# Attention in pairs of steps instead of single steps, in a fused attention and feed-forward block

## The reference, cut to what matters

```python
q = (layernorm(x) @ Wq + bq).reshape(8, 512, 16, 16)      # B, S, H, DK
k = (ctx @ Wk + bk).reshape(8, 512, 16, 16)
v = (ctx @ Wv + bv).reshape(8, 512, 16, 16)
scores = einsum('bqhd,bkhd->hbqk', q, k) / sqrt(16)
attn = softmax(scores.reshape(16 * 8, 512, 512), axis=0)  # over head and batch together
out = einsum('hbqk,bkhd->bqhd', attn.reshape(16, 8, 512, 512), v)
x = x + tanh(g_xattn) * (out @ Wo + bo)
x = x + tanh(g_ffn) * ffn(layernorm(x))                   # quantised, 704 wide
```

## Time and profile before

| | us |
|---|---|
| median of 3 runs | 893.19 (891.55 to 894.06) |
| the profiled execution | 890.11 |
| its span, first to last instruction | 888.3 |
| attention stage, first scores (312.9) to last value products (742) | 429 |
| mean granted TensorE clock | 0.973 of full speed |

### The profile page before, as it was taken

How to read it: one execution, slowest core, us unless ns; L and a number is a source line. 1 busy time by engine, 2 the same in 40 slices (tenths; PEclk the granted TensorE clock), 3 DMA queues, 4 the chain that set the end, 5 groups by cost and what they waited for, 6 DMA issues and landing times. The chain is left out here.

```text
span 888.3 us, 20668 instructions
## 1 busy us (share of the span) xinstructions
PE 770.7 (87%) x8127; PEld 438.8 (49%) x8149; DVE 781.0 (88%) x1001; ACT 706.7 (80%) x1095; POOL 494.9 (56%) x353
## 2 busy tenths in 40 slices
PE   8897887877777688999889999999999989948977
PEld 6563361112212155666556666666666657714434
DVE  4799539999999979999799999999999995767968
ACT  3454449999999878899788999999999952768973
POOL 1333463000000017999898999999999996514500
PEclk9999999999999989999999999999999989969999
DMA  9796786565555567778776786768857566200014
GB/s 299 262 315 203 245 240 130 138 167 140 140 139 130 202 183 228 239 225 265 231 227 211 234 265 191 212 174 259 259 164 211 168 225 192 91 1 1 0 43 148
DMA packets 98094, 164.34 MB, mean 185 GB/s; under 512 B 9616, under 2 KB 37008, under 8 KB 97680
## 3 DMA queue, kind: packets, MB, share of 16 engines
q1 hardware_dynamic: 98000, 163.03, 61.5%
HBM read 133.63 MB, written 41.94 MB: 198 GB/s over the span
## 5 line engine op out<-in xcount | busy, mean ns | idle before, releaser
L978 POOL TENSOR_TENSOR e<-e,recip 128x768 f32<-128x768 f32 (+3 forms) x256 | 387.4, 1558 | 34.6 <-DVE recip L1020 34.6
L928 ACT ACTIVATE e<-ps_att 128x512 f32<-128x512 f32 x512 | 302.0, 648 | 36.6 <-PE ps_att L869 35.6
L1009 DVE TENSOR_REDUCE pair_sums<-e 128x128 f32<-128x2048 f32 x128 | 291.6, 2281 | 20.0 <-ACT e L928 19.6
L869 PE MATMUL ps_att<-arena 128*128 128x128 bf16 x2048 | 192.7, 220 | 0.3 <-issue 0.2
L884 PE MATMUL acc<-e,arena 128*32 128x128 f32 x4096 | 179.5, 294 | 11.7 <-DVE e L990 4.2
L869 PEld LDWEIGHTS ps_att<-arena 128*128 128x128 bf16 x2048 | 151.0, 98 | 58.8 <-issue 3.6
L694 ACT ACTIVATE copies<-ps_max 128x1024 bf16<-128x1024 f32 x189 | 175.6, 1087 | 0.0
L865 PE MATMUL ps_att<-shift,minus 128*128 128x512 bf16 x394 | 154.2, 391 | 14.9 <-DMA arena<-k_stack 9.2
L884 PEld LDWEIGHTS acc<-e,arena 128*32 128x32 f32 x4096 | 106.6, 111 | 40.7 <-POOL e L978 10.9
L709 DVE TENSOR_TENSOR high<-copies,high 128x3072 bf16<-128x3072 bf16 x63 | 110.0, 1745 | 0.4 <-ACT copies L694 0.4
L961 POOL CAST bo_parts<-arena 96x256 bf16<-96x256 f32 x1 | 0.4, 394 | 175.5 <-DMA arena<-in_L_xattn_bo_dram 175.5
(11 more groups left out here) (162 smaller groups left out, 879.0 us busy)
## 6 DMA issues: line engine op xcount, KB each, us to landing
arena<-k_stack SPq DMA_DIRECT2D x256, 256.0 KB, 3.3
arena<-q_stack SPq DMA_DIRECT2D x64, 256.0 KB, 4.2
k_stack<-parts SPq DMA_DIRECT2D x40, 256.0 KB, 3.5
q_stack<-parts SPq DMA_DIRECT2D x40, 256.0 KB, 3.6
k_stack<-k_stack SPq DMA_DIRECT2D x12, 512.0 KB, 10.9
arena<-in_x_dram SPq DMA_DIRECT2D x5, 1024.0 KB, 8.7
arena<-in_ctx_dram SPq DMA_DIRECT2D x4, 1024.0 KB, 6.5
arena<-q_stack SPq DMA_DIRECT2D x8, 512.0 KB, 8.0
```

The costliest lines, as they stand in the source:

```text
L869: last = nc.tensor.matmul(bank[:, j * P:(j + 1) * P], ks[:, i % KRING, b * P:(b + 1) * P], qs[:, h, b * P:(b + 1) * P], start=False, stop= ...
L928: nc.scalar.activation(e_at(qc * STEPS + i, half * HB, (half + 1) * HB).rearrange("p q b i -> p b q i"), ps[(qc * (2 * STEPS) + 2 * i + ha ...
L978: nc.gpsimd.tensor_tensor(part, part, by_pairs(recip[:, kc % 2, :], share), ALU.mult).then_inc(pool_scaled, 1)
L1009: nc.vector.tensor_reduce(pair_sums[:, :, h // 2, :], e[:, g % RING // 2].rearrange("p q s b i -> p q i (s b)"), AX.X, ALU.add).then_inc(s ...
```

## The change

- The unit of PE's order, of the ring, of the scaling and of the semaphores becomes the pair. PE does the four halves of two steps' scores, then the products of a whole pair (16 f32 matmuls, 32 records), 10 pairs behind. `e` is a ring of 11 pairs: the same memory and the same addresses within it.
- DVE and POOL scale a pair with one instruction each: POOL 8 blocks of 16 in the first pair of a region, 12 in the seventh, else 13; in the last region 6.
- DVE sums two pairs in one instruction, three times a region, and one pair twice, where a group of two would run over the ring's end one by one; the last sum has 5 or 6 parts instead of 8. DVE scales ahead of each sum, 8 pairs after the pair's exponentials.
- ACT's copies of `acc` stand behind pairs 4, 6, 8 and 10 of a chunk instead of steps 10, 14, 18 and 22.
- The shift of every fourth half is written by ACT as before, from the same half on.

```diff
-    LAG = 20
-    SLAG = 17
-    RING = 22
+    CHUNK = NC * PAIRS
+    ALL_PAIRS = NC * CHUNK
+    LAG = 10
+    RING = 11
+    BLOCKS = 2 * B
...
-    GATHER_AT = [LAG - H + BANK_HEADS * (j + 1) + 2 for j in range(BANKS)]
+    BANK_PAIRS = BANK_HEADS // 2
+    GATHER_AT = [LAG - PAIRS + BANK_PAIRS * (j + 1) for j in range(BANKS)]
...
-        return 7 if i % 4 == 1 else 6
+    POOL_BLOCKS = (8, 13, 13, 13, 13, 13, 12, 13)
+    END_BLOCKS = 6
+    GROUPS = ((0, 1), (2, 3), (4, 5), (6,), (7,))
+    def pool_share(p):
+        return END_BLOCKS if p >= ALL_PAIRS - PAIRS else POOL_BLOCKS[p % PAIRS]
...
-    FIRST_PRESET = 2 * LAG + 3
+    FIRST_PRESET = 4 * LAG + 3
...
-        e = sb("e", [P, RING // 2, QP, 2, B, 2])
-        pair_sums = sb("pair_sums", [P, QP, PAIRS, 2])
+        e = sb("e", [P, RING, QP, BLOCKS, 2])
+        partial = sb("partial", [P, QP, len(GROUPS) + 1, 2])
...
-                    for i in range(STEPS):
-                        for half in range(2):
-                            scores(qc, i, half)
-                        if LAG <= i < LAG + H and (i - LAG) % BANK_HEADS == 0:
-                            j = (i - LAG) // BANK_HEADS
+                    for j in range(CHUNK):
+                        for half in range(4):
+                            scores(qc, 2 * j + half // 2, half % 2)
+                        if LAG <= j < LAG + PAIRS and (j - LAG) % BANK_PAIRS == 0:
+                            bank = (j - LAG) // BANK_PAIRS
                             if not first:
-                                pe.wait_ge(gathered, BANKS * (qc - 1) + j + 1)
-                            clear(j)
-                        if i >= LAG or not first:
-                            for half in range(2):
-                                times_v(qc * STEPS + i - LAG, half)
+                                pe.wait_ge(gathered, BANKS * (qc - 1) + bank + 1)
+                            clear(bank)
+                        if j >= LAG or not first:
+                            times_v(qc * CHUNK + j - LAG)
...
+                        if p >= RING:
+                            act.wait_ge(multiplied, p - RING + 1)
+                        for half in range(4):
+                            n = 4 * p + half
+                            act.wait_ge(scored, n + 1)
                             nc.scalar.activation(
-                                e_at(qc * STEPS + i, half * HB, (half + 1) * HB).rearrange("p q b i -> p b q i"),
+                                e_at(p, half * HB, (half + 1) * HB).rearrange("p q z i -> p z q i"),
...
                             if preset(n + SCORES):
                                 act.wait_ge(exped, n + 1)
...
+                def add_up(p, n, k):
+                    dve.wait_ge(exped, 4 * (p + n))
+                    t = p % RING
+                    nc.vector.tensor_reduce(partial[:, :, k, :], e[:, t:t + n].rearrange("p t q z i -> p q i t z"),
+                                            AX.XY, ALU.add).then_inc(sum_done, 1)
...
+                for r in range(NC * NC):
+                    for k, (p, n) in enumerate(groups(r)):
...
+                            if p % PAIRS < PAIRS - 1:
+                                for i in range(n):
+                                    scale(p + i - PAIRS)
+                                if p % PAIRS + n == PAIRS - 1:
+                                    scale(p + n - PAIRS)
+                        add_up(p, n, k)
+                    invert(r, len(list(groups(r))))
```

More of the change, by code:

```diff
@@ L872, in scores, with times_v @@
                     last.then_inc(scored, 1)
[L874 to L888, removed]
+                def times_v(p):
+                    pe.wait_ge(pool_scaled, p + 1)
+                    pe.wait_ge(dve_scaled, p + 1)
+                    kc, pair = p % CHUNK // PAIRS, p % PAIRS
+                    for odd in range(2):
+                        for b in range(B):
+                            col = (pair * 2 + b // HB) * P
+                            grp = 32 * (b % HB)
+                            v_col = pair * 3 * DK + DK * odd
+                            z = odd * B + b
+                            last = nc.tensor.matmul(acc[grp:grp + 32, col:col + P], vpad[:, kc, b, v_col:v_col + 32],
+                                                    e_at(p, z, z + 1), start=False, stop=False,
+                                                    skip_group_check=True)
+                    last.then_inc(multiplied, 1)
                 def clear(j):
@@ L909, in _ @@
                     chunk(qc, False)
-                for g in range(ALL - LAG, ALL):
-                    for half in range(2):
-                        times_v(g, half)
+                for p in range(ALL_PAIRS - LAG, ALL_PAIRS):
+                    times_v(p)
             @block.scalar
@@ L921, in chunk @@
                 def chunk(qc, first):
[L922 to L927, removed]
-                            nc.scalar.activation(
-                                e_at(qc * STEPS + i, half * HB, (half + 1) * HB).rearrange("p q b i -> p b q i"),
[L930 to L933, removed]
+                    for j in range(CHUNK):
+                        p = qc * CHUNK + j
+                        if p >= RING:
[3 more added lines that the diff above has]
+                            act.wait_ge(scored, n + 1)
+                            nc.scalar.activation(
+                                e_at(p, half * HB, (half + 1) * HB).rearrange("p q z i -> p z q i"),
+                                ps[n % SCORES][:].rearrange("p (z q i) -> p z q i", z=HB, i=2),
+                                ACT.Exp, scale=DK ** -0.5).then_inc(exped, 1)
                             if preset(n + SCORES):
@@ L1024, in _, with scale @@
[L1024 to L1029, removed]
+                def scale(p):
+                    r = p // PAIRS
+                    if p % PAIRS == 0:
+                        dve.wait_ge(recip_copied, r + 1)
+                    share = pool_share(p)
+                    part = e_at(p, share, BLOCKS)
+                    nc.vector.tensor_tensor(part, part, by_pairs(recip_v[:, (r % 2) * P:(r % 2 + 1) * P], BLOCKS - share),
+                                            ALU.mult).then_inc(dve_scaled, 1)
@@ L1032, in ffn @@
+                for p in range(ALL_PAIRS - PAIRS, ALL_PAIRS):
+                    scale(p)
 def ffn(nc, sem, x, out_parts, out, keep):
```

100 lines of the change are left out of this document (41 added, 59 removed).

## The result

The changed kernel takes 933.62 us (930.14 to 934.12) against 892.54 for the kernel before in the same measurements: a ratio of 1.045, 95% interval 1.042 to 1.047. That is 41.1 us slower. The forecast was 945, 52.5 more than before, with a range from 929 to 958. The profiled execution of the changed kernel took 934.12, that of before 890.11.

What follows compares the result with a forecast made beforehand. Bound: a loop over PE and ACT, 3.12 us a pair; the moved half adds 0.50, so 3.62 x 117 = 423.5, with disturbances 435.8 against 383.35; with drain +52.7 on 890.1 to 893.19, forecast 945, range 929 to 958.

Steps and rivals of the forecast that it cites:

- The bound: Attention stage: a loop over PE and ACT through ACT's shift copy sets the pair, 3.10 us, 3.12 measured.
- The moved half of the products: First-step products, 16 records, move behind the last quarter of scores onto the loop: 0.50 us a pair, 0.41 to 0.77.
- s0: First of the four quarters of a pair's scores on PE; starts the loop, 0.71 us before E0.
- The pair: Attention stage, loop period of one pair (two steps): 3.12 + 0.50 = 3.62 us, times 117 = 423.5.
- E0: ACT's exponential of s0; the shift copy stands right behind it, counted 0.70 us later in the loop.
- Disturbances: Window beyond the loop: clears 3.3, filling 2.0, late K tiles 6, others 1 us; 18.3 before the change.
- Turns: PE's switches between scores and products: one each way a pair goes, where PE waits anyway; priced at 0.
- region starts: Starts of 8-pair regions, where products wait for scaled numbers: those stalls go, 2.5 us on DVE alone before.
- rival C: DVE's two-pair sums run at half the rate: 4.9 us a pair, near 1090 us; chance 0.03.
- rival A: Work of the engines is the pace, POOL fullest at 2.94 us a pair: faster, 865 us; chance 0.05.
- Rival B: PE's clock falls as PE idles about 0.7 us in each pair: about 1020 us; chance 0.05.
- Drain: End of the attention stage, POOL's last scalings and the last products: nothing moves much, +0.2 us.

Runs made afterwards that it cites:

- e2: Kernel before with only PE's order changed: four quarters of scores, then the products of two steps; 930.36 us, ratio 1.043.
- e4: Changed kernel with ACT's shift copy moved behind the pair's second exponential, for the next pair's first quarter; 877.94 us, ratio 0.985.
- e6: Changed kernel with the products of each pair's first step computed a second time, between second and third quarter of scores; 941.69 us, ratio 1.057.
- e9: Kernel before with ACT's shift copy moved behind the second exponential, for the next pair's first quarter; 882.12 us, ratio 0.987.
- e3: Changed kernel without ACT's copy of the shift, PE writing every shift; 886.18 us, ratio 0.992.
- e8: Kernel before without ACT's copy of the shift, PE writing every shift; 899.62 us, ratio 1.008.
- e1: Changed kernel with PE's old order, first-step products back between second and third quarter of scores; scaling, sums and ring by pairs; 897.59 us, ratio 1.008.
- e7: Like e6, but the second computation reads a fixed tile, 128 numbers in a row, instead of the ring; 931.96 us, ratio 1.045.
- e10: Like e7, but the fixed tile is read in the ring's own steps, 64 pieces 128 bytes apart; 932.76 us, ratio 1.046.

## Why the prediction was right, and where it was off

- **The bound.** Right: a loop over PE and ACT through the copy of the shift. e2 shows it with PE's order alone, e4 by moving the copy alone, and e6 by giving PE 23% more work for 8 us. In the kernel before the loop bound by little: with the copy moved there, most pairs took 3.00 to 3.03 (e9) instead of 3.12.
- **The moved half of the products.** Forecast 0.50, measured 0.49 (1.12 instead of 0.63 from products to s0). The nearest row, products behind products in the drain, was the right price. The stated high end, 0.77, did not go into the range, which took 0.55 without a reason; with 0.77 its upper end would have been some 26 us higher.
- **The pair.** Forecast 3.62, measured 3.56: the term that was mis-sized. The step "0.71 + 0.70 + 0.60 + 0.15 + 0.31 + 0.63" was carried over with its 0.70 from E0 to S. That number contained a slowdown of E0 by the very products that the change takes away from beside it; it became 0.65. 0.06 x 117 = 7 us of the 11 too many. What E0 gained there the last exponential lost: E3, now beside the products, has a median of 0.68 instead of 0.63 over pairs 11 to 126, but it is not on the loop. ACT's waits for scores, forecast near 76, came to 85.2.
- **Disturbances.** Forecast 12.3 in the window, measured 425.15 - 117 x 3.56 = 8.6. Waits for late K tiles are down from 9.7 to 3.8 (the earlier trace rows counts weight loads, and so does this row of the changed kernel; I had kept 6):

```profile
PEld ps_att L882 <- DMA arena<-k_stack: 3.8, 3, 1.6
```

  Filling: pair 10 lasted 6.20 (forecast 5.6). A clear costs 0.22 (pairs of 3.78 instead of 3.56), as priced.
- **Turns, DVE, POOL, ring, region starts.** All priced at nothing under the longer loop: right, no engine is over 85% busy in the window, and from 342 on the products never wait for DVE. A two-pair sum takes 4.42, less than two of 2.28; rival C did not come true. The rule of the Trainium skill (VectorE: DVE Perf Modes, section on the TRN2 errata), that larger tiles save their fixed part, agrees with 2 x 2.28 - 4.42 = 0.14 a merged sum; it decided nothing while the loop was the bound, as rival A would have needed.
- **Rival B, the clock.** The granted clock was 1.00 in mid-stage with PE idle 0.62 in each pair. Within the window it fell only in pairs 10 and 11, to 0.83 and 0.84: PE sat idle 1.62 before the products of pair 10 (the view names DVE, but the scaling that ended last, at 341.16, was POOL's), and the shift after them took 0.61 instead of 0.39. The oscillation that the Trainium skill describes for banks used in turn (TensorE: Matmul & The Clock Gate, section on psum-queue depth-cycling) does not show at these gaps in mid-stage.

```profile
341.22 1.93 PE L902 MATMUL acc<-e,arena 128*32 128x128 f32 x32 [1.62 <-DVE e L1002]
343.09 0.61 PE L882 MATMUL ps_att<-shift,minus 128*128 128x512 bf16 x1
```

- **Drain.** Forecast +0.2, measured -0.2.
- **The base.** I had added nearly all of the 3.1 us by which the profiled execution of before lay under its median. That of the changed kernel lies at its median's upper side (934.12 against 933.62), so the profiled executions differ by 44.0, the medians by 41.1. Of the 44.0, the window has 41.8; 2.3 lie behind the attention stage, where 148.25 us passed instead of 145.94 although the change touches nothing there. That the window alone comes so near to the 41.1 of the medians is in part chance.

## What to carry to other kernels

When all engines look 90% full, follow one period of the timeline from an instruction back to itself: each step from one release to the next is a term, and as long as that loop sets the pace only work on it has a price. Merging steps to save turns or fixed costs can move work from beside a wait to behind it. So look first for the wait that the merged work would land behind, here that for a 0.6 us copy by another engine. Moving that copy to where its result is needed one period later made the kernel before 0.9 to 1.3% faster and the changed kernel about 6%. The change by pairs itself cost 4.5% with the copy where it was, gained 1.5% without any copy (e3 against e8), and could not be told from nothing with the copy moved.

## What the runs showed of the hardware

The first exponential of a pair (128x512 f32, from PSUM into the ring in SBUF) had a median of 0.69 to 0.71 us over pairs 11 to 126 where it ran beside products that read the ring (before, e1, e6), and of 0.62 to 0.63 beside products that read another tile (e7, e10) or beside none (the changed kernel). It was worth 8 us in 933 (e6 against the changed kernel; 10 against e7), since E0 was on the loop. What is shared, no run shows. The Trainium skill (SBUF — State Buffer, section "Who interferes with whom") says that PE and ACT never wait on anyone. Read so that an exponential lasts as long whatever PE reads, these measurements differ from it, and they decide for this case.
